# Attention inside a sandwich layer on one core: probability-value products two query steps at a time, float32r scores with one full-row stack, and a batch loop written out

## What is computed

```python
x = x + 0.5 * ffn(layernorm(x))
x = x + attn(layernorm(x))
x = x + 0.5 * ffn(layernorm(x))
# ffn: base product, plus one of 8 adapters (256->64->256), chosen per batch by
#      the least reconstruction error of 8 encoders (256->64) and decoders (64->256)
# attn: 16 heads of 16 features, q and k rotated,
#       softmax(q k^T / 4) v per head, and an output product
```

## Time and profile before

| | |
|---|---|
| median of 3 runs | 2005.18 us (2001.39 to 2006.41) |
| profiled execution | 2006.59 us, span 2004.8 us |
| PE busy | 1820.8 us, 91% |
| DVE busy | 1272.4 us, 63% |
| ACT busy | 988.0 us, 49% |
| POOL busy | 504.2 us, 25% |
| hardware queue q1 | 26.1% of 16 engines |

### The profile page before, as it was taken

How to read it: one execution, slowest core, us unless ns; L and a number is a source line. 1 busy time by engine, 2 the same in 40 slices (tenths; PEclk the granted TensorE clock), 3 DMA queues, 4 the chain that set the end, 5 groups by cost and what they waited for, 6 DMA issues and landing times.

```text
span 2004.8 us, 29856 instructions
## 1 busy us (share of the span) xinstructions
PE 1820.8 (91%) x9128; PEld 996.1 (50%) x9128; DVE 1272.4 (63%) x2795; ACT 988.0 (49%) x1954; POOL 504.2 (25%) x663
## 2 busy tenths in 40 slices
PE   6598999999899998999989999899989999998885
PEld 4344545454454645455454545446445464545244
DVE  5476767676566765667657676666747676764631
ACT  1246554546555453555535555454545545464541
POOL 1404142131413213141311414122141422313101
PEclk9698999999999998999989999999989999999797
DMA  4504124050501405032240503206050140605000
GB/s 108 96 13 78 26 44 74 12 106 12 100 8 43 74 12 106 12 70 37 43 75 12 106 3 71 45 12 106 12 104 4 45 72 12 106 1 102 5 12 11
DMA packets 96817, 99.79 MB, mean 50 GB/s; under 512 B 19974, under 2 KB 88327, under 8 KB 96519
## 3 DMA queue, kind: packets, MB, share of 16 engines
q1 hardware_dynamic: 93896, 97.19, 26.1%
q10 hardware_dynamic: 2752, 0.54, 0.2%
HBM read 63.54 MB, written 33.55 MB: 48 GB/s over the span
## 4 chain that ended last, share of the span: by engine, by line
PE 63%; DVE 9%; DMA 9%; issue 8%; ACT 4%; SPq 3%; POOL 2%; POOLq 0%; DVEq 0%; ACTq 0%
PE ps L520 10%; PE ps L508 9%; PE ps L496 8%; PE ps L587 8%; PE ps L566 6%; DMA scratch<-parts 5%; DVE mx L838 5%; PE ps L575 4%; PE ps L624 4%; SPq L481 3%; DMA out_dram<-x 3%; PE ps L642 3%; PE ps L687 2%; ACT pr L722 2%; PE ps L627 2%
## 5 line engine op out<-in xcount | busy, mean ns | idle before, releaser
L838 DVE TENSOR_REDUCE mx<-ps 128x1 f32<-128x512 f32 x1024 | 655.2, 685 | 277.4 <-PE ps L496 274.6
L722 ACT ACTIVATE pr<-ps 128x512 f32<-128x512 f32 x1024 | 555.9, 598 | 288.1 <-PE ps L508 287.6
L496 PE MATMUL ps<-stack 96*128 96x512 bf16 x1024 | 329.2, 391 | 59.8 <-issue 36.4
L508 PE MATMUL ps<-stack 98*128 98x512 bf16 x1024 | 322.7, 387 | 18.6 <-ACT pr L722 9.8
L520 PE MATMUL ps<-pr,va 128*32 128x512 f32 x2048 | 275.2, 610 | 4.6 <-ACT pr L722 4.6
L777 ACT ACTIVATE h<-ps,benc 128x512 f32<-128x512 f32 x128 | 88.0, 687 | 254.8 <-PE ps L566 254.8
L508 PEld LDWEIGHTS ps<-stack 98*128 98x128 bf16 x1024 | 77.7, 100 | 271.3 <-ACT pr L722 174.1
L496 PEld LDWEIGHTS ps<-stack 96*128 96x128 bf16 x1024 | 97.4, 99 | 221.9 <-DVE mx L838 88.1
L890 DVE SCALAR_TENSOR_TENSOR ps<-ps,wb,h 128x512 f32<-128x512 f32 x128 | 96.7, 756 | 138.4 <-PE ps L575 138.4
L1035 POOL TENSOR_SCALAR rs<-mv 128x4 f32<-128x4 f32 x48 | 11.2, 232 | 646.1 <-DVE mv L858 640.4
L575 PE MATMUL ps<-h,gram_w 128*128 128x512 f32 x256 | 132.5, 599 | 0.0
(11 more groups left out here) (155 smaller groups left out, 2983.9 us busy)
## 6 DMA issues: line engine op xcount, KB each, us to landing
stack<-scratch SPq DMA_DIRECT2D x384, 128.0 KB, 4.4
scratch<-parts SPq DMA_DIRECT2D x64, 384.0 KB, 5.6
xin<-in_L_attn_x_dram SPq DMA_DIRECT2D x16, 512.0 KB, 3.5
out_dram<-x SPq DMA_DIRECT2D x16, 512.0 KB, 6.1
stack<-wu_mT SPq DMA_DIRECT2D x128, 4.0 KB, 1.7
cst<-in_const_dram SPq DMA_DIRECT2D x1, 1024.0 KB
raw<-in_L_ffn_W_dec_dram ACTq DMA_DIRECT2D x1, 512.0 KB, 5.8
pr<-in_L_ffn_W_enc_dram SPq DMA_DIRECT2D x2, 256.0 KB, 7.8
```

The lines of the kernel that those rows point to most:

```text
L496: pe.matmul(bank1[:, t % 2, :], stack[b.odd][0][0:KB, hd, 128 * t:128 * t + 128], stack[b.odd][1][0:KB, hd, :], start=True, stop=True).the ...
L508: pe.matmul(bank2[:, a % 2, :], stack[b.odd][1][:, 4 * g + a, 128 * t:128 * t + 128], stack[b.odd][0][:, 4 * g + a, :], start=True, stop=T ...
L722: act.activation(pr[:, n % 2, a, :], bank2[:, a % 2, :], ACT.Exp, scale=SCALE).then_inc(ex_done.sem, 1)
L838: dve.tensor_reduce(mx[:, hd // 4 % 2, e:e + 1], bank1[:, t % 2, :], AX.X, ALU.max).then_inc(mx_done.sem, 1)
```

## The change

1. The bf16 parts become two float32r parts, high and low. Three part products are stacked (48 rows a head). The key stack holds two heads at once, in partitions 0 to 47 and 64 to 111; the query stack has 112 rows as well, with zeros under the other head. Both are held once, so the loads for the next batch wait for the exponentials of this one (`ex_done(b - 1, ...)`). Rows 112 and 113 take the maxima; all of the key stack starts as -1.
2. `rest` (POOL) and `middle` (ACT) go. The high part is put to the scratch by itself (`put_high`), and its four loads are issued while the low part is on its way; two loads follow. Three buffers for parts go round. Four q and k parts still take six loads each, and two puts instead of one.
3. The transposition of the maxima becomes a float32 product with the identity.
4. `pr` has four buffers instead of two, and the PV products of two query steps are issued together in each odd step from 7 on.
5. The loop over batches is written out.
6. Once at the start: GpSimd fills the key stack, ScalarE fills the query stack with zeros in two pieces (`w3`).

```diff
-BLOCKS = 6
-KB = BLOCKS * HD
-Q_PARTS = (0, 0, 1, 0, 2, 1)
-K_PARTS = (0, 1, 0, 2, 0, 1)
+BLOCKS = 3
+HALF = 64
+TOP = HALF + BLOCKS * HD
+Q_PARTS = (0, 1, 0)
+K_PARTS = (0, 0, 1)
+HI_SLOT = (0, 2, 1, 0)
+LO_SLOT = (1, 0, 2, 1)
...
-                if 6 <= s < 22 and half == (s < 21): step("pv", i, s - 6)
+                if 7 <= s < 22 and s % 2 and half == (s < 21):
+                    step("pv", i, s - 7)
+                    step("pv", i, s - 6)
...
-    for i in (-1, 0, 1):
-        known(i)
-    trips = (B - 4) // 2
-    with engine.Fori(0, trips) as k:
-        one(2, k * 2 + 2, 0)
-        one(3, k * 2 + 3, 1)
-    for i in range(2 + 2 * trips, B + 1):
+    for i in range(-1, B + 1):
         known(i)
...
-        parts = [sb(f"parts{k}", [128, 3, S], BF16) for k in range(2)]
-        stack = [[sb(f"stack{o}{a}", [KB + 2, H, S], BF16) for a in range(2)] for o in range(2)]
+        parts = [sb(f"parts{k}", [128, S], FR) for k in range(3)]
+        stack_q = sb("stack_q", [128, H, S], FR)
+        stack_k = sb("stack_k", [128, H // 2, S], FR)
-        pr = sb("pr", [128, 2, 4, S])
+        pr = sb("pr", [128, 4, 4, S])
...
+            def put_high(b, k):
+                sp.wait_ge(*hi_done.at(b, k))
+                sp.dma_start(scratch[b.odd][k][:, :, 0, :].rearrange("h d n -> (h d) n"), parts[HI_SLOT[k]][:].bitcast(F32))\
+                    .then_inc(hi_put[k].sem, 16)
+            def spread(b, k, part):
+                m = 4 * (k // 2)
+                for j, p in enumerate((Q_PARTS, K_PARTS)[k % 2]):
+                    if p == part:
+                        for e in range(2):
+                            rows = slice(HALF * e + HD * j, HALF * e + HD * j + HD)
+                            dst = stack_k[rows, m:m + 4, :] if k % 2 else stack_q[rows, 2 * m + e:2 * m + 8:2, :]
+                            sp.dma_start(dst.bitcast(F32),
+                                         scratch[b.odd][k].rearrange("(h e) d a n -> e d h a n", e=2)[e, :, :, part, :])\
+                                .then_inc(stacked[k].sem, 16)
             def stack_up(b, k):
                 sp.wait_ge(*lo_done.at(b, k))
+                sp.dma_start(scratch[b.odd][k][:, :, 1, :]..., parts[LO_SLOT[k]][:].bitcast(F32)).then_inc(lo_put[k].sem, 16)
+                sp.wait_ge(*ex_done.at(b - 1, H * T * (k // 2 + 1) // 2 - 1))
+                sp.wait_ge(*hi_put[k].at(b, 0))
+                spread(b, k, 0)
+                sp.wait_ge(*lo_put[k].at(b, 0))
+                spread(b, k, 1)
...
-                    pe.matmul(bank1[:, t % 2, :], stack[b.odd][0][0:KB, hd, 128 * t:128 * t + 128],
-                              stack[b.odd][1][0:KB, hd, :], start=True, stop=True).then_inc(s1_full.sem, 1)
+                    pe.matmul(bank1[:, t % 2, :], stack_q[0:TOP, hd, 128 * t:128 * t + 128],
+                              stack_k[0:TOP, hd // 2, :], start=True, stop=True).then_inc(s1_full.sem, 1)
...
-                pe.transpose(bank[0:32, 0:64].bitcast(BF16), mx2[:, g % 2, :, :].rearrange("p a b -> p (a b)"),
-                             ident_b[:]).then_inc(mt_full.sem, 1)
+                pe.matmul(bank[0:32, 0:128], mx2[:, g % 2, :, :].rearrange("p a b -> p (a b)"), ident,
+                          start=True, stop=True).then_inc(mt_full.sem, 1)
...
-                    act.wait_ge(*pv_done.at(b, n - 2))
+                    act.wait_ge(*pv_done.at(b, n - 4))
...
-            def middle(b, k):
-                act.wait_ge(*rest_done.at(b, k))
-                act.copy(parts[k % 2][:, 1, :], qb[k % 2][:]).then_inc(mi_done.sem, 1)
+            def zeros(m):
+                act.activation(stack_q[:, 8 * m:8 * m + 8, :], v["cos"][:, 0:S].unsqueeze(1).to_broadcast([128, 8, S]),
+                               ACT.Copy, scale=0.0).then_inc(s_zero, 1)
...
-            def rest(b, k):
-                q = qb[k % 2]
-                pool.wait_ge(*hi_done.at(b, k))
-                pool.tensor_tensor(q[:], q[:], parts[k % 2][:, 0, :], ALU.subtract).then_inc(rest_done.sem, 1)
```

More of the change, by code:

```diff
@@ L157, in dense @@
                 step("pick", n, 0)
-                if initial(n): step("w2")
+                if initial(n):
+                    step("w2")
+                    step("w3", 0)
             if at == (8, 0): step("dn", n, 0)
@@ L161, in dense @@
             if at == (11, 1): step("st", n, 2, 0)
[L162 removed]
+            if at == (12, 0):
+                step("up", n, 0, 1)
+                if initial(n): step("w3", 1)
             if at == (12, 1):
@@ L331, in macaron @@
         oT = qs
-        scratch = [[nc.dram_tensor(f"scratch{o}{k}", [8, HD, 3, S], BF16, kind="Internal").ap() for k in range(4)]
+        scratch = [[nc.dram_tensor(f"scratch{o}{k}", [8, HD, 2, S], F32, kind="Internal").ap() for k in range(4)]
                    for o in range(2)]
@@ L457, in _ @@
                 bring(s_rest, b0_bc[:], b0.partition_broadcast(128))
-                sp.wait_ge(s_fill, 1)
-                for o in range(2):
-                    bring(s_rows, stack[o][1][KB:KB + 2, :, :].rearrange("p h (a x) -> p (h a) x", x=2 * 128),
-                          minus.unsqueeze(1).to_broadcast([2, 2 * H, 2 * 128]))
             def store(b):
@@ L474, in stack_up @@
             def stack_up(b, k):
                 sp.wait_ge(*lo_done.at(b, k))
-                sp.wait_ge(*ex_done.at(b - 2, H * T - 1))
-                sp.dma_start(scratch[b.odd][k].rearrange("h d a n -> (h d) a n"), parts[k % 2][:]).then_inc(put_done[k].sem, 16)
-                sp.wait_ge(*put_done[k].at(b, 0))
-                for j, part in enumerate((Q_PARTS, K_PARTS)[k % 2]):
-                    sp.dma_start(stack[b.odd][k % 2][HD * j:HD * j + HD, 8 * (k // 2):8 * (k // 2) + 8, :],
-                                 scratch[b.odd][k][:, :, part, :].rearrange("h d n -> d h n")).then_inc(stacked[k].sem, 16)
@@ L484, in _ @@
-            walk(sp, dict(load=load, store=store, mt=maxima, ro3=stack_up))
+                sp.dma_start(scratch[b.odd][k][:, :, 1, :].rearrange("h d n -> (h d) n"), parts[LO_SLOT[k]][:].bitcast(F32))\
+                    .then_inc(lo_put[k].sem, 16)
+                if initial(b):
+                    sp.wait_ge(s_fill, 1)
+                    sp.sem_inc(passed, 1)
+                    sp.wait_ge(s_zero, k // 2 + 1)
+                sp.sem_inc(passed, 1)
+                sp.wait_ge(*ex_done.at(b - 1, H * T * (k // 2 + 1) // 2 - 1))
@@ L485, in _ @@
+                sp.sem_inc(passed, 1)
+                sp.wait_ge(*hi_put[k].at(b, 0))
+                spread(b, k, 0)
+                sp.wait_ge(*lo_put[k].at(b, 0))
+                spread(b, k, 1)
+            walk(sp, dict(load=load, store=store, mt=maxima, ro2=put_high, ro3=stack_up))
             sp.wait_ge(*stored.at(Batch(B - 1, 1), 0))
@@ L507, in s2 @@
                     pe.wait_ge(*ex_done.at(b, 4 * n + a - 2))
-                    pe.matmul(bank2[:, a % 2, :], stack[b.odd][1][:, 4 * g + a, 128 * t:128 * t + 128],
-                              stack[b.odd][0][:, 4 * g + a, :], start=True, stop=True).then_inc(s2_full.sem, 1)
+                    pe.matmul(bank2[:, a % 2, :], stack_k[0:TOP + 2, 2 * g + a // 2, 128 * t:128 * t + 128],
+                              stack_q[0:TOP + 2, 4 * g + a, :], start=True, stop=True).then_inc(s2_full.sem, 1)
             def pv(b, n):
@@ L734, in maxima @@
                 bank = late
-                if initial(b) and g == 0:
-                    act.wait_ge(s_rows, 32)
                 act.wait_ge(*mt_full.at(b, g))
                 act.wait_ge(*mq_done[g % 2].at(b, g // 2 - 1))
-                act.copy(mT[:, g % 2, :], bank[0:32, 0:64].bitcast(BF16)).then_inc(mT_done.sem, 1)
+                act.copy(mT[:, g % 2, :], bank[0:32, 0:128]).then_inc(mT_done.sem, 1)
             def normalise(b, s, half):
@@ L810, in _ @@
             do = dict(s2=s2, pv=pv, mt=maxima, lx=normalise, tr=transposed, en=encode, dn=down, qk=project,
-                           ro2=high, ro3=middle, ot=out_transposed)
+                           ro2=high, ot=out_transposed, w3=zeros)
             act.dma_start(w_dec, W_dec.rearrange("(a b) r d -> (b r) a d", b=2)).then_inc(s_decoder, 16)
```

47 lines of the change are left out of this document (23 added, 24 removed).

## The result

| kernel | median us | runs | profiled execution | ratio to before |
|---|---|---|---|---|
| before | 2005.80 (2001.39 to 2007.71) | 4 | span 2004.8 | 1 |
| changed | 2034.83 (2033.64 to 2042.98) | 4 | 2033.64, span 2031.6 | 1.0157, 95% interval 1.0125 to 1.0188 |

The changed kernel is slower by 29 us (25 to 38 us by the interval). The forecast was 2016.5 (its own terms add up to 2016.2), slower by 11: the sign is right, the time lies inside the range (1978 to 2036) at its upper end, and the size is off by 18 us.

What follows compares the result with a forecast made beforehand. TensorE's stream bounds most half-steps, with ScalarE's exponentials and VectorE's maxima just under it. Fourteen batches at +3.0 (+42), batch 0 +3.5, batch 15 +8, start -6.5, edges -36: +11, median 2016.5 us, range 1978 to 2036.

Steps and rivals of the forecast that it cites:

- loop edges: Batch loop's back edges: five stops of all engines go when it is written out, -36 us; bounds -36 and 0.
- pairing, a steady batch: PV blocks moved into odd half-steps: those lengthen by 6.0 us, even ones gain 3.1; net +2.7, bounds -1.7 and +3.1.
- float32r scores: Score matmuls on TensorE: 15 ns more for each of 104, plus dearer entries, +1.7 us a batch; bounds 0 and 1.8.
- maxima's product: Float32 product with the identity replacing the bf16 transpose of the maxima: +0.7 us a batch; bounds 0.3 and 1.
- rest and middle: Two rotation links removed: low part goes 1.8 us earlier, last PV bank's copy waits for PV alone, -1.1 a batch.
- store: Output store on SP's queue goes some 3 us earlier, ahead of most loads: -0.95 us a batch; bounds 0 and -1.05.
- before the first batch: Unhidden chain of four parts, 1.8 us less each, less some overlap: -6.5 us; bounds -3 and -7.
- The rival that counts TensorE's stream alone: Pairing gives -1.7 a batch instead of +2.7; even half-steps without PV shrink under 1.2 us; 1950 us, chance 0.12.
- five entries behind a PV pair: Within the float32r score term: 0.1 us for five score entries following paired PV blocks.
- the rival built on it (1987 us): Score weight loads are hidden under the running matmul, so float32r is free: 1987 us, chance 0.20.
- SyncE's order: SP queue: high part put ahead, four loads while the low part flies, store some 3 us earlier: -0.95 a batch.
- the light half-steps: Even half-steps left without PV: 10.1, 12.1 and 14.1 at 1.6 to 1.8 us instead of 1.97, behind ScalarE and VectorE.

Runs made afterwards that it cites:

- run 1: Kernel before with only its batch loop written out: 1973.11 us, ratio 0.9816.
- run 9: Kernel before with only its batch loop written out, measured a second time: 1977.34 us, ratio 0.9845.
- run 8: Changed kernel with PV products one by one except product 2 joined to 3 at 9.1, three exponential buffers, seven part buffers, one maxima transposition: 1965.13 us, ratio 0.9802.
- run 10: Changed kernel with the puts of the high parts and the output store issued from ScalarE's queue instead of SyncE's: 2025.61 us, ratio 1.0086.
- run 7: Changed kernel with each batch's first PV product back in step 6, the second alone at 7.1, others paired: 2021.51 us, ratio 1.0081.
- run 4: Changed kernel, still paired, with both score products reading a constant bfloat16 tile instead of the float32r stacks: 1994.50 us, ratio 0.9927.
- run 6: Changed kernel with the maxima turned by one float32 transposition instead of the product with the identity: 2013.45 us, ratio 1.0044.
- run 2: Changed kernel with PV products issued one step at a time, as in the kernel before: 2001.09 us, ratio 0.9946.
- run 5: Changed kernel with PV products one by one and both score products on the constant bfloat16 tile: 1953.20 us, ratio 0.9738.
- run 3: Changed kernel with PV products one by one, two exponential buffers instead of four and eight part buffers instead of three: 1994.77 us, ratio 0.9933.
- run 12: The kernel of run 8 with the output store alone moved to ScalarE's queue: 1958.48 us, ratio 0.9756.

## Why the prediction was right in sign and short in size

| term, us | forecast | measured | by |
|---|---|---|---|
| loop edges | -36 | -37, -31 | runs 1, 9 |
| pairing, a steady batch | +2.7 | +1.7 in float32r, +2.2 in bf16 | table, 6.0 to 20.0 |
| float32r scores | +1.7 | +2.4 in pairs, +2.9 one by one | table, and 0.38 in steps 0 to 5 where nothing stalls |
| half-clock stretches | none | +0.55 | five of 1.53 in 14 batches |
| maxima's product | +0.7 | +0.7 | 8.0 and three like it, 0.18 each |
| rest and middle | -1.1 | -1.2 | last s2 to next |
| store | -0.95 | -0.5 | steps 0.1 and 1.0 |
| before the first batch | -6.5 | 0 (-3.9 in run 8) | 89.4 to 89.5 (85.6) |

Taking pairing as it is in float32r and the format as it is one by one, the steady batch comes to 1.7 + 2.9 + 0.55 + 0.7 - 1.2 - 0.5 = +4.1 us, and 4.0 were measured.

**The loop.** Right in place and size.

**Pairing.** The mechanism stood in the earlier trace rows and was right: a block added to an odd half-step costs 0.84 to 0.86 us (0.85 forecast), 8.1 gives 1.12 back (1.1), 10.1 gives 0.19 (0.16). In 6.1, 16.1 and 18.1, 0.09, 0.66 and 0.28 came (0.2, 0.5 and 0.5 forecast). But 12.1 and 14.1 give 0.53 (0.3) and half of it goes again, as 13.0 grows by 0.30 and 15.0 by 0.25; why the light ones came out 0.2 us shorter than worked out was not traced. These are differences from the kernel before, with the dearer weight loads in them, as in the forecast; by pairing alone the even half-steps give more (12.1: 2.12 to 1.44), which is why it costs 1.7 us and not 2.7. The rival that counts TensorE's stream alone falls all the same: it wanted even half-steps under 1.2 us. The Trainium skill (TensorEngine Tiling (Array Packing), Key Properties) says that a change of tiling mode drains the array. The trace agrees with some 0.24 us a pair, and the runs show that this saving is not what decides: pairs cost 38 to 42 us by the ratios and 30 to 40 by the profiles.

**float32r scores: the step that was mis-sized.** "0.1 us for five entries behind a PV pair, and leave 0.4 us under present waits." The entry costs 0.11 us behind every PV block, alone or in pairs, and the 0.4 us that were to be hidden do not show: even 3.1, without a block, grew by 0.22. Five entries were counted, and there are sixteen blocks in a batch, or eight pairs. By the ratios the format costs 42 to 46 us where 1.7 x 14 and some 6 at the ends, 30, had been put. The Trainium skill (TensorE: Matmul & The Clock Gate, Step-by-step) has the next weights loading while a matmul runs. Products in a row bear that out as far as 14 to 18 ns each, 0.23 apart with loads of 190 ns. Behind a PV block the 0.11 us are about what the load is dearer by (188 against 98 ns), so there it does not look hidden, and the rival built on it (1987 us) is refuted by the 42 to 46 us.

**SyncE's order: the step whose mechanism was wrong.** "In the new order the high part is put ahead, four loads go while the low part flies ... The store goes some 3 us earlier", and with it, before the first batch, "nothing hides this chain: four parts with 1.8 us less each", -6.5. The new functions were costed as if each started when its data is ready. On an in-order queue the high put of a part stands behind the loads of the part before, which wait for a landing. Ahead of the first batch the same queue held VectorE, since three part buffers make a low part wait for a high one to land. TensorE's transposes (L571) wait for VectorE's copy of the values (L955), which stands behind the last low part. Timeline of the changed kernel, VectorE, then TensorE:

```profile
78.21 1.30 DVE L972 TENSOR_TENSOR parts<-qb,parts 128x512 fp32r<-128x512 f32 x1 [2.93 <-DMA scratch<-parts]
86.50 0.69 DVE L972 TENSOR_TENSOR parts<-qb,parts 128x512 fp32r<-128x512 f32 x1 [6.99 <-DMA scratch<-parts]
87.11 1.28 DVE L955 TENSOR_TENSOR va<-ps,bv_bc 128x512 f32<-128x512 f32 x2
...
87.89 1.94 PE L571 MATMUL ps<-cst,xn 128*128 128x128 f32 x8 [13.15 <-issue]
```

With a buffer for each part (run 8) the same rows read:

```profile
80.25 1.28 DVE L955 TENSOR_TENSOR va<-ps,bv_bc 128x512 f32<-128x512 f32 x2
81.03 1.94 PE L571 MATMUL ps<-cst,xn 128*128 128x128 f32 x8 [6.81 <-issue]
...
85.61 1.19 PE L518 MATMUL ps<-stack_k,stack_q 112*128 112x512 f32 x2 [2.64 <-issue]
```

VectorE's path is now 6.9 us earlier (6.6 against the kernel before, where the copy of the values starts at 86.84), what was forecast, but the first score product comes only 3.9 earlier and stands idle for 2.64. In the program nothing is left for it to wait for but the stack loads of parts 0 and 1; the second of these leaves SyncE at 77.57, where the kernel before had it leave at 80.35. So the forecast had one path where there are two, and the one through SyncE got shorter by less. Forecast were -6.5 here and -0.95 x 14 = -13.3 for the store. Nothing of the first and some 7 of the second came, and run 10 brings some 9 back (3.8 here, 5.3 in steps 0 and 1).

**The clock.** The forecast had no term for it: "the light half-steps" were priced by waits alone. Run 7 shows that the stretches come with the emptied step 6.

**The sum.** By the steady batches: float32r +1.2, clock +0.55, store +0.45, pairing -1.0 and rest -0.1 make +1.1 us a batch; measured are 1.0, 14 us in all; the start adds 6.5; batches 0 and 15 were put 5 too high. Together +16 on a span forecast of +11, and +26.8 were measured. Part of what was missed in one term was covered by another, so the small miss in the total flatters the working.

## What to carry to other kernels

Cost a new transfer at the place where its queue reaches it, not when its data is ready: write down what each item of the in-order queue waits for, and follow every path to the first product, not only the longest one of today. A block of work that one stream no longer has at a step is worth only what the next wait leaves, and where it had filled a step, its absence can bring a lower granted clock behind it. A format's price is paid at every entry behind another form of product, so count entries, not only products.

## What the runs showed of the hardware beyond that

- A granted clock of 0.50 for 3.4 us inside steady batches, 1.53 us each, with TensorE 93% busy over the span. It takes little to go: product 0 (run 7, none), the bfloat16 scores (run 4, none), one transposition (run 6, one left of five), each seen in one profiled execution. Runs 1, 2, 5, 8 and 9 show some as well, at step 1.0 of single batches (batch 2 in run 2), behind a step 0.1 that the wait for the output store has made 1.6 to 3 us longer. But as long a step 0.1 is also seen with no stretch behind it (batch 2 of run 1), so the lull goes before them and does not by itself bring them.
- A transposition of a 32-column float32 tile costs less in its half-step than the bfloat16 transposition of the kernel before (8.0: 2.44 us against 2.59), though both are one matmul record each and the float32 one is the longer (273 against 230 ns). Why stays open.
- TensorE's start-up differs between executions. Timeline of TensorE in the profile of run 1, then in that of run 9, the same kernel:

```profile
22.34 0.63 PE L560 MATMUL ps<-xl,w_eh 128*128 128x512 f32 x1
22.77 0.62 PE L560 MATMUL ps<-xh,w_eh 128*128 128x512 f32 x1
23.20 0.42 PE L560 MATMUL ps<-xh,w_el 128*128 128x512 f32 x1
```

```profile
18.37 0.40 PE L560 MATMUL ps<-xh,w_el 128*128 128x512 f32 x1
18.60 0.40 PE L560 MATMUL ps<-xl,w_eh 128*128 128x512 f32 x1
```

The encoder's first products come 0.43 us apart up to 23.20 us in the one, and 0.23 apart from 18.37 on in the other. The first batch starts at 93.4 and 88.6, and batch 0 takes 108.3 and 104.7 us; the profiled executions are 1977.28 and 1967.94 us long. Runs 1, 2, 3, 5 and 12 were profiled with the late start-up (in 2 and 5 it lasts some 3 us longer than in 3), the others with the early one; that is why the readings by batch stand beside the ratios above, which mix both kinds of execution. What decides it was not tried.
